# Second and last attention: the scale goes into the query, and the maximum is written negated by the reduction

## The reference

```python
s = jnp.einsum('bhqd,bhkd->bhqk', q, k) * SCALE
p = jax.nn.softmax(s, axis=-1)
return jnp.einsum('bhqk,bhkd->bhqd', p, v)
```

## Time and profile before

| what | us |
|---|---|
| median of 3 executions | 2489.25 |
| lowest and highest of them | 2482.87 and 2489.47 |
| span of the profiled execution (first to last instruction) | 2529.0 |
| second attention, its 128 steps | about 515 to 912 |
| last attention, its 64 steps | about 2009 to 2284 |

### The profile page before, as it was taken

How to read it: one execution, slowest core, us unless ns; L and a number is a source line. 1 busy time by engine, 2 the same in 40 slices (tenths; PEclk the granted TensorE clock), 3 DMA queues, 4 the chain that set the end, 5 groups by cost and what they waited for, 6 DMA issues and landing times.

```text
span 2529.0 us, 37538 instructions
## 1 busy us (share of the span) xinstructions
PE 2145.7 (85%) x11277; PEld 1490.0 (59%) x11277; DVE 1335.8 (53%) x3670; ACT 1135.0 (45%) x3508; POOL 964.9 (38%) x879
## 2 busy tenths in 40 slices
PE   6999999788898887979999999788999587873682
PEld 4666666656676654646666566444666366652572
DVE  2545554477777644346565555242333777773233
ACT  4444444345545544335666565332333266661231
POOL 1212111033344334544443636312555303445574
PEclk9999999989999988989999999899999689996796
DMA  9999300200000032650000000233665332232598
GB/s 351 358 350 344 114 1 1 67 1 1 1 19 11 8 87 55 104 132 1 1 1 1 36 1 36 75 112 97 104 104 97 84 83 88 90 95 77 129 189 192
DMA packets 223567, 233.93 MB, mean 92 GB/s; under 512 B 35803, under 2 KB 215267, under 8 KB 222604
## 3 DMA queue, kind: packets, MB, share of 16 engines
q1 hardware_dynamic: 186124, 183.40, 24.1%
q0 software_dynamic: 37248, 48.14, 10.6%
HBM read 95.60 MB, written 143.85 MB: 95 GB/s over the span
## 4 chain that ended last, share of the span: by engine, by line
PE 47%; issue 28%; DVE 11%; DMA 5%; ACT 4%; SPq 2%; POOL 2%; another core or an unknown queue 1%; POOLq 0%; DVEq 0%; ACTq 0%
PE ps L129 39%; PE ps L920 2%; DMA moe_sum<-xn,work 1%; PE ps L1893 1%; DMA work<-f_rows 1%; PE ps L1908 1%; DVE n_mx L1014 1%; ACT work L2614 1%; PE ps L578 1%; DVE xn L247 1%; DMA moe_sum<-work 1%; DVE weights L1188 1%; DMA f_sum<-work 1%; DVE n_mx L2701 1%
## 5 line engine op out<-in xcount | busy, mean ns | idle before, releaser
L129 PE MATMUL ps<-weights,work 128*128 128x126 f32 (+6 forms) x3188 | 630.5, 334 | 37.7 <-ACT weights L2623 26.4
L129 PEld LDWEIGHTS ps<-weights,work 128*128 128x128 f32 (+2 forms) x3188 | 454.6, 196 | 89.7 <-issue 45.6
L129 PE MATMUL ps<-work,weights 128*128 128x512 f32 (+3 forms) x1408 | 483.3, 468 | 3.2 <-ACT work L668 3.1
L129 PE MATMUL ps<-xn_T,weights 128*128 128x512 f32 (+5 forms) x960 | 363.3, 512 | 24.5 <-DVE qvar L723 8.4
L129 PEld LDWEIGHTS ps<-work,weights 128*128 128x128 f32 (+2 forms) x1408 | 213.8, 186 | 86.4 <-issue 74.8
L1971 POOL DMA_INDIRECT f_sum<-work x120 | 185.3, 1544 | 183.1 <-ACT work L1932 158.4
L743 POOL TENSOR_TENSOR work<-work,rinv 128x512 f32<-128x512 f32 x128 | 133.3, 1041 | 299.4 <-DVE rinv L694 277.0
L129 PEld LDWEIGHTS ps<-xn_T,weights 128*128 128x128 f32 (+3 forms) x960 | 151.7, 192 | 122.8 <-issue 101.7
L1039 POOL TENSOR_TENSOR work<-weights,head_sel 128x512 f32<-128x512 f32 x128 | 134.5, 1055 | 223.7 <-PE ps L129 198.0
L989 ACT ACTIVATE work<-ps,n_negm 128x128 f32<-128x128 f32 x512 | 145.2, 371 | 146.2 <-DVE n_negm L1016 143.5
L3015 POOL DMA_INDIRECT f_rows<-ctx,weights x128 | 125.3, 979 | 188.0 <-DVEq L3104 119.9
(11 more groups left out here) (333 smaller groups left out, 3617.8 us busy)
## 6 DMA issues: line engine op xcount, KB each, us to landing
f_rows<-weights SPq DMA_DIRECT2D x25, 2176.0 KB, 19.6
work<-f_rows SPq DMA_DIRECT2D x120, 136.0 KB
weights<-in_L_ffn_gate_up_proj SPq DMA_DIRECT2D x29, 384.0 KB, 7.4
f_rows<-weights SPq DMA_DIRECT2D x4, 2592.0 KB, 23.9
work<-f_rows SPq DMA_DIRECT2D x64, 162.0 KB
f_sum<-weights SPq DMA_DIRECT2D x4, 2176.0 KB, 16.5
weights<-in_L_ffn_W SPq DMA_DIRECT2D x96, 88.0 KB
moe_sum<-weights SPq DMA_DIRECT2D x3, 2176.0 KB, 17.9
```

What stands on the lines that cost most here:

```text
L129: return nc.tensor.matmul(out, lhsT, rhs, start=start, stop=stop, skip_group_check=True)
```

## The change

It does four things in either attention:

- The reduction writes the negated maximum directly (`negate=True`) into `n_negm`. The tile `n_mx`, the multiplication by -scale and the chained wait between the two are gone: 128 instructions in the second attention, 64 in the last.
- The exponential no longer has a scale, so that it is exp(score + n_negm).
- In the second attention the scale is applied by the copy that reorders the query's weights (`l1_wqs`), once. In the last it is applied to the vectors qn_w and qn_b (`l3_vec[:, 0:2]`) as they are copied from PSUM; one copy of 10 columns becomes two, of 2 and 8.
- The wait for the exponentials of step t - 4 stands ahead of the reduction now, since this writes the ring's slot.

```diff
--- before.py
+++ after.py
@@ -834,7 +834,6 @@
 
     n_p = tile(WK, 0, 2048).rearrange("p (n h k) -> p n h k", n=4, h=NB)
     n_pt = tile(WK, 2048, 1024).rearrange("p (n c) -> p n c", n=2)
-    n_mx = sb("n_mx", [P, 4, 2 * NB])
     n_negm = sb("n_negm", [P, 4, 2 * NB])
     n_rinv = sb("n_rinv", [P, 32])[:]
     S_BANKS = (B4, B5, B3)
@@ -864,7 +863,7 @@
             self.needs_qk, self.needs_v = {}, {}
             self.tail_t = tail_t
             n = self.n
-            self.chain = signal("attn_chain", n + TB)
+            self.chain = signal("attn_chain", TB)
             self.kblk_ready = signal("narrow_kblk_ready", n)
             self.s_mm = signal("attn_s_mm", n)
             self.negm_ready = signal("attn_negm_ready", n)
@@ -951,7 +950,7 @@
         if not S.new:
             out_product()
 
-    def slim_act(act, S, scale, o_t, beside):
+    def slim_act(act, S, o_t, beside):
         A, s = S.A, S.s
 
         def out_of_y(n, k):
@@ -987,7 +986,7 @@
                 done(act, A.pt_tr, s, t - 4)
                 for j in range(NB):
                     last = nc.scalar.activation(n_p[:, i, j, :], S_BANKS[t % 3][:, j * P:(j + 1) * P], ACT.Exp,
-                                                bias=n_negm[:, i, j:j + 1], scale=scale)
+                                                bias=n_negm[:, i, j:j + 1])
                 last.then_inc(A.p_ready.sem, 1)
             if S.tail and t - A.tail_t in (4, 5):
                 tail_act(act, S.n, S.prev, t - A.tail_t - 4)
@@ -996,7 +995,7 @@
             for k in range(KD):
                 out_of_y(tail_of(A.stage, s)[0], k)
 
-    def slim_dve(dve, S, scale, beside):
+    def slim_dve(dve, S, beside):
         A, s = S.A, S.s
         link = S.chain(dve, A.chain, 1, s)
         for t in S.steps:
@@ -1011,10 +1010,9 @@
                                         n_rinv.unsqueeze(2).broadcast_to([P, A.heads, A.hd]), ALU.mult).then_inc(A.on_ready.sem, 1)
             if S.new:
                 done(dve, A.s_mm, s, t)
-                link(nc.vector.tensor_reduce(n_mx[:, t % 4, 0:NB], S_BANKS[t % 3].rearrange("p (h k) -> p h k", h=NB), AX.X, ALU.max))
                 done(dve, A.p_ready, s, t - 4)
-                nc.vector.tensor_scalar(n_negm[:, t % 4, 0:NB], n_mx[:, t % 4, 0:NB], -scale, None, ALU.mult)\
-                    .then_inc(A.negm_ready.sem, 1)
+                nc.vector.tensor_reduce(n_negm[:, t % 4, 0:NB], S_BANKS[t % 3].rearrange("p (h k) -> p h k", h=NB), AX.X, ALU.max,
+                                        negate=True).then_inc(A.negm_ready.sem, 1)
             u = t - P_LAG
             if u % 2 and S.has(u):
                 done(dve, A.pt_tr, s, u)
@@ -2342,7 +2340,7 @@
     dca_ready = signal("narrow_v_ready", 2, 1)
     dk_in = [Signal(semaphore(f"l3_dk_in{i}"), 16, B // 2, 0) for i in range(2)]
     dv_in = [Signal(semaphore(f"l3_dv_in{i}"), 16, B // 4, 0) for i in range(4)]
-    l3_chain = signal("attn_chain", STEPS + 2 * STEPS // 2, 1)
+    l3_chain = signal("attn_chain", 2 * STEPS // 2, 1)
     l3_s_mm = signal("attn_s_mm", STEPS, 1)
     l3_negm = signal("attn_negm_ready", STEPS, 1)
     l3_p = signal("attn_p_ready", STEPS, 1)
@@ -2414,7 +2412,8 @@
     def l3_setup_act(act):
         act.wait_ge(in_l3x, 16 * L3_LOADS)
         act.wait_ge(vec_tr.sem, vec_tr.value(0, 0))
-        nc.scalar.activation(l3_vec, B7[:, 0:10], ACT.Copy).then_inc(vec_ready.sem, 1)
+        nc.scalar.activation(l3_vec[:, 0:2], B7[:, 0:2], ACT.Copy, scale=SCALE3)
+        nc.scalar.activation(l3_vec[:, 2:10], B7[:, 2:10], ACT.Copy).then_inc(vec_ready.sem, 1)
 
     def l3_setup_dve(dve, link):
 
@@ -2612,7 +2611,7 @@
                     for j in range(NB):
                         m = x * NB + j
                         last = nc.scalar.activation(n_p[:, i, j, lo:hi], S_BANKS[t % 3][:, j * P + lo:j * P + hi], ACT.Exp,
-                                                    bias=n_negm[:, i, m:m + 1], scale=SCALE3)
+                                                    bias=n_negm[:, i, m:m + 1])
                 last.then_inc(l3_p.sem, 1)
             u = t - O_LAG
             if u % 2 and 0 <= u < STEPS:
@@ -2697,11 +2696,10 @@
             if 0 <= t < STEPS:
                 done(dve, l3_s_mm, 0, t)
                 bank = S_BANKS[t % 3].rearrange("p (h k) -> p h k", h=NB)
+                done(dve, l3_p, 0, t - 4)
                 for x, lo, hi in ((0, 0, MAIN), (1, MAIN, P)):
-                    ins = nc.vector.tensor_reduce(n_mx[:, t % 4, x * NB:(x + 1) * NB], bank[:, :, lo:hi], AX.X, ALU.max)
-                link(ins)
-                done(dve, l3_p, 0, t - 4)
-                nc.vector.tensor_scalar(n_negm[:, t % 4, :], n_mx[:, t % 4, :], -SCALE3, None, ALU.mult).then_inc(l3_negm.sem, 1)
+                    ins = nc.vector.tensor_reduce(n_negm[:, t % 4, x * NB:(x + 1) * NB], bank[:, :, lo:hi], AX.X, ALU.max, negate=True)
+                ins.then_inc(l3_negm.sem, 1)
             u = t - P_LAG
             if u % 2 and 0 <= u < STEPS:
                 done(dve, l3_pt_tr, 0, u)
@@ -3365,14 +3363,15 @@
         for s in range(0, NS):
             ffn0_act(act, 1, s)
         act.wait_ge(in_l1x, 16 * 5)
-        nc.scalar.activation(l1_wqs.rearrange("p k (t n) -> p k t n", t=2), l1_wq.rearrange("p k (n t) -> p k t n", t=2), ACT.Copy)
+        nc.scalar.activation(l1_wqs.rearrange("p k (t n) -> p k t n", t=2), l1_wq.rearrange("p k (n t) -> p k t n", t=2), ACT.Copy,
+                             scale=float(L1HD) ** -0.5)
         nc.scalar.activation(l1_wks.rearrange("p (t n) -> p t n", t=2), l1_wkv[:, 0:D].rearrange("p (n t) -> p t n", t=2), ACT.Copy)
 
         nc.scalar.activation(l1_bias[:], l1_bias[:], ACT.Copy, scale=gates[:, 1:2]).then_inc(l1w_ready, 1)
         act.wait_ge(l1w_ready, 1)
         act.wait_ge(pool_consts, 2)
         rope = rope_act(act)
-        run_ahead(lambda S: slim_act(act, S, float(L1HD) ** -0.5, l1_ot, rope), L1, act)
+        run_ahead(lambda S: slim_act(act, S, l1_ot, rope), L1, act)
         act.wait_ge(gqk_ready, 1)
         first_keys_act(act, L2, lambda u: between_act(act, u))
         tiles_run(lambda g, new, old: tiles_act(act, F1, g, new, old), F1, act)
@@ -3412,7 +3411,7 @@
         for s in range(0, NS):
             ffn0_dve(dve, 1, s)
         rope = rope_dve(dve)
-        run_ahead(lambda S: slim_dve(dve, S, float(L1HD) ** -0.5, rope), L1, dve)
+        run_ahead(lambda S: slim_dve(dve, S, rope), L1, dve)
         dve.wait_ge(in_l2x, 16 * 5)
 
         nc.vector.scalar_tensor_tensor(gqk[:], gqk[:], SCALE_WIDE, gk[:], ALU.mult, ALU.mult).then_inc(gqk_ready, 1)
```

## The result

| | us |
|---|---|
| before, median of 4 on the same chip | 2487.78 (2482.87 to 2489.47) |
| after, median of 4 | 2451.91 (2448.35 to 2459.41) |
| after / before | 0.9859, 95% interval 0.984 to 0.9879 |
| predicted | 2477 (2465 to 2490), 0.995 |

The kernel is 35.9 us faster. The profiled execution of after took 2454.56 us and spans 2452.8. Its span must not be set against the 2529.0 of before: the experiments will make it likely that this is a span from a slower chip.

What follows compares the result with a forecast made beforehand. TensorE was taken to set most of the second attention, its idle time waiting on VectorE's copies. Gains of 7.3 us (second attention) and 4.8 (last), 12.1 in all, off 2489.25 gave 2477 us, range 2465 to 2490.

Steps and rivals of the forecast that it cites:

- The view of what binds: Both attentions: TensorE sets most of the second; savings return only from its idle time, 42.5 and 53.8 us.
- The removed multiplication: On the chain: 0.19 us a place, 38 places or 7.2 us in the second attention, 31 or 5.9 in the last.
- the first rival: VectorE after each reduction: no overlap, so a place gives 0.11 us; 2482 us, chance 0.10.
- The wait inside it: The multiplication's wait for GpSimd, both attentions: together 2.5 us on the chain; most of the 22 us excess lies off it.
- TensorE busy as before with 35 idle: Second attention's profile after: 128 steps take about 390 us instead of 397, with TensorE's busy time unchanged.
- I keep two thirds, 4.8: Last attention: DMA loads and the 15.65 us end stall swallow some gain; of 7.2 us, 4.8 kept.
- the two-input instructions: Second attention: VectorE instructions with two SBUF operands take over GpSimd's waits at most places, losing a third of the gain.
- The second rival: Last attention's gain all swallowed, a third of the second's lost; gain about 5 us, 2484 us, chance 0.20.
- Negation and scale: Both attentions: negating in the reduction and moving the scale each taken as 0 us.
- the doubled wait on the reduction: Reduction has two semaphores instead of one: 0.06 us at 19 places where TensorE releases it, 1.1 us lost.
- The third rival: VectorE leaving crowded stretches earlier also shortens waits the chain doesn't show; about 22 us, 2467 us, chance 0.14.

Runs made afterwards that it cites:

- spare: Changed kernel plus an unchained multiplication on unused data behind each reduction, nobody waiting for it; 2513.26 us against before's 2526.82, ratio 0.9942.
- port: Kernel before with scale folded into the query and the multiplication replaced by a chained one-element negating reduction, both attentions; 2506.95 us, ratio 0.9924 to before.
- spare_red: Changed kernel plus an unchained one-element reduction on unused data behind each reduction; 2498.69 us against before's 2525.21, ratio 0.99.
- after_third: Changed kernel, no further edit, timed once more on another chip; 2492.63 us against before's 2525.21, ratio 0.9884.
- again: Kernel before, unchanged, as a control with a second profile; 2528.02 us against 2526.72, ratio 1.0001.
- only4: Kernel before with the change's edits in the last attention only; 2520.57 us against 2526.72, ratio 0.9978.
- after_again: Changed kernel, no further edit, timed again on another chip; 2497.12 us against before's 2526.82, ratio 0.9876.

## Why the prediction was wrong

**The view of what binds** held. The stage, the engine that is late and TensorE's wait for the copies were the right ones: in the second attention the wait has 23.7 to 28.4 us in the four profiles with the old pair, 21.7 in spare, 18.1 in port, 14.7 in spare_red and 15.7 in after_third, which is the order of their times but for the last two, whose times aren't told apart.

**"The removed multiplication", 0.19 us a place**, held. Reduction to next start is 0.60 us where it was 0.80, and the overlap is there: the first rival (0.69) is out. The Trainium skill's exception to the DRAIN rule (VectorE: DVE Perf Modes, "Two Vector instructions with no wait between them") is what 0.60 against an instruction of 0.69 shows. With the chained wait this is the 11 us by which the change beats `port`, against 13.1 - 1.1 = 12.0 in the sum; the intervals leave that 11 uncertain by several us.

**"The wait inside it", 2.5 us on the chain, is the step that failed.** By `port` it is worth 19 us with its consequences. I had noted from the chain only the waits that stood there under the name `n_negm`. The chain books most of them under "issue". Before at 2016, its timeline and then its chain (start, us):

```profile
2016.67 1.75 DVE L2704 TENSOR_SCALAR n_negm<-n_mx 128x8 f32<-128x8 f32 x1
2018.34 0.68 DVE L2724 TENSOR_TENSOR weights<-ps,weights 128x512 f32<-128x512 f32 x1
```

```profile
2016.67 0.06 DVE n_negm L2704
2016.73 1.60 issue
2018.34 0.69 DVE weights L2724
```

The instruction is 1.75 us long, and the chain gives 0.06 to it and 1.60 to nothing recorded. The same stands at the place of the earlier trace rows:

```profile
681.69 0.06 DVE n_negm L1016
681.75 0.23 issue
681.98 0.68 DVE weights L1183
```

Over the same 38 and 31 places, the timeline of before has 15.4 and 11.2 us from the end of the reduction to the start of the next instruction, 0.08 of overlap a place included. Of the 11.2 a copy has 1.6 that waited for something else:

```profile
2257.69 0.69 DVE L2709 COPY work<-ps 128x512 f32<-128x512 f32 x1 [1.50 <-remote]
```

That leaves 9.6. The sum had 7.2 + 0.9 = 8.1 and 5.9 + 1.6 = 7.5. So the direct terms should have been 25.0 us and not 15.6. The profile of before alone held that; I read one view of it too literally. Even these are more than came back as idle time of TensorE, 13.3 of the 15.4 and 3.5 of the 9.6.

**"TensorE busy as before with 35 idle"** was the second error: busy fell by 7.9 and 3.4 us, idle to 29.0 in the second attention, below the 35 forecast. Each long stall that is shortened may also spare TensorE a stretch at 1.2 GHz. I took a us of stall for a us of time. At the place shown it was 0.6 us directly and 1.7 by the clock. That is no rule for every place: of the four profiles with the old pair in the second attention and the copies as before, two show the fall there (before, again), of the ten others none. Less time at the lower level is measured, and it accounts for the fall in busy time; that the shorter stalls cause it is my reading of this order of events, and no run held the one fixed while the other moved.

**"I keep two thirds, 4.8"**, in the last attention, is neither borne out nor refuted: `only4` gains 6 us by the times, with an interval from 1 to 10, and the profiles have 6.9, half of it busy time. The stall of 15.65 us didn't swallow it, since it is about as long in the repeats. Nor did "the two-input instructions" take over the waits: between the same exponentials those with two operands in SBUF are busy for 41.1 to 44.5 us in the four old profiles and 41.4 to 42.3 in the four new. L1158 has 692 ns, where the same line of before, L1160, had 825; L1186 has 637, and L1188, its line before, 604 in before and 633 in again. Those with one operand in SBUF took over a little, 41.0 us before and 44.6 to 45.0 after, 4 us of the 22 that the multiplication had waited. The second rival is out.

**The bounds.** Negation and scale cost 0 as taken. No run isolates the doubled wait on the reduction; the prediction's 1.1 us for it is not tested. The third rival (22 us, 2467) came nearest, for the reason that it gave in half: it had the mechanism of relieved stretches, without the clock.

**What stays open.** The profile of after on the first chip has no stall behind the last scores, where before and the repeats have 14 to 16 us. After, and then after_again, in the chain (start, us):

```profile
2225.49 0.45 PE ps L2596 x4
2225.95 0.02 issue
2225.97 0.61 ACT xn_T L2679
```

```profile
2261.96 15.92 another core or an unknown queue
2277.90 0.61 ACT xn_T L2679
```

It is the same program, so the stall's absence isn't of the change. Whether it is of the chip can't be told, since no profile of before on that chip was taken. And the first chip's ratio, 0.9859, isn't told apart from 0.988.

## What to carry to other kernels

A tiny VectorE instruction from SBUF to SBUF is not tiny beside a busy GpSimd: look at its mean against its shortest (340 against 170 ns here), and write it as a reduction, or away. To price what a stretch of the chain costs, take the distance from one instruction's start to the next in the timeline, because the chain can call an engine's wait for GpSimd "issue". And where a saving shortens stalls of TensorE, read its busy time in both profiles too: here 11 of 28 us came from the clock.

## What was not expected of the hardware

The same kernel took 2487.78 us on one chip and medians of 2525.2 to 2526.8 on three others; the span of a profile from one of them can't be set against times from another. A stretch that the change doesn't touch, between the two attentions, takes 1090 us in after on the first chip, and 1103 and 1104 in its two repeats. The first of these and the last:

```profile
887.00:1977.00 1090.00, 973.51 (x4639) 627.18 (x4638) 526.62 (x1507) 486.03 (x1326) 485.80 (x423) 0.95 0.29 65
```

```profile
882.00:1985.00 1103.00, 977.51 (x4637) 628.42 (x4636) 526.33 (x1507) 485.93 (x1325) 485.92 (x423) 0.94 0.29 64
```

TensorE accounts for 4 of the 13 us; the rest is idle time, and what causes it on the slower chips was not pursued.
